# Expert weights in four wide pieces per expert through a raw ring of four slots

## The chip, the cores and the metric

The kernel runs on one core of a Trainium2 chip. The metric is the device time of one execution in microseconds. Lower is better. A core has a matrix engine (TensorE, PE), an engine for element-wise work and reductions (VectorE, DVE), one for activations (ScalarE, ACT), one for custom work (GpSimd, POOL) and one that here only issues DMAs (SyncE, SP). Each runs its own queue of instructions in order, and they meet at semaphores.

## What is computed

One layer with the norm behind each half, over 2048 tokens of width 512, in fp32:

```python
x = layernorm(x + attention(x, W_K, W_Q, W_V, W_O))      # 16 heads of 128, causal
logits = x @ gate_w.T                                    # 64 experts
gate_vals, idx = top_k(softmax(logits), 6)
xe = the tokens of each expert, at most 128              # [64, 128, 512]
h  = silu(xe @ w1.T) * (xe @ w3.T)                       # [64, 128, 352]
ye = h @ w2.T                                            # [64, 128, 512]
routed = sum over the 6 of gate_vals * ye
z  = silu(x @ sw1.T) * (x @ sw3.T) @ sw2.T               # shared expert, 704 wide
x  = layernorm(x + routed + z)
```

## The kernel before

Four stages follow each other, each with its own block of queues: attention, projection and routing, the experts, and the combination of their results. The edit lies in the third, the function `experts`.

Every fp32 matrix operand is split into a high part (rounded to the matrix engine's format) and a low part (what is left), and a product takes three passes: high by high, low by high, high by low. For weights ScalarE makes the high part with a copy (`split_piece`, L1363) and VectorE the low part with a subtraction (L1470). Both read the raw weights from a ring in SBUF, `raw` (named `w_raw` in the trace), which SP fills (L1305).

The stage has eight bodies, and each body has twelve units in the order e, e, s: two experts and one half of the shared expert for one tile of 128 tokens. So there are 32 groups of three units in all. In a unit u TensorE does this in order: it transposes h of the unit before (`turn`, L1560), computes `up` (L1584, 24 matmuls of 352 columns), transposes the tokens of the next unit if that is an expert (L1555), and computes `down` of the unit before (L1607, 9 matmuls of 512 columns). At the start of a body, unit 0's own tokens are transposed only there, ahead of its `up`.

In a unit ScalarE splits the transposed h (L1386, L1387), writes out the result of the unit before last (L1399, and the store L1402; for a finished shared tile the store L1408), then splits the first pieces of the step, does Silu (L1427), splits the transposed tokens of the next unit into `eT` (L1381), and splits the remaining pieces. VectorE follows in the same order with the low parts, and where ScalarE does Silu it multiplies the halves into `h_sb` (L1520); `eT_lo` (L1488) comes behind it. For every second shared unit it first adds the finished tile (L1465). `up` waits for `eT_lo` and for the last up piece of its expert (`w_lo`), `turn` waits for `h_sb`, and `down` waits for the last down piece.

Before, an expert has seven pieces: four up pieces of 128 x 704 words (w1 and w3 together, one for each 128 of the 512 input columns) and three down pieces of 512 columns on 128, 128 and 96 rows. They are spread over the steps of a group (e is the group's first expert) so:

```python
pieces_of_step += [[(e + 1, p) for p in UP[2:]] + [(e, p) for p in DOWN],
                   [(e + 1, p) for p in DOWN] + [(e + 2, p) for p in UP[:2]],
                   [(e + 2, p) for p in UP[2:]] + [(e + 3, p) for p in UP[:2]]]
```

The first three pieces of each step are split ahead of Silu (`mine[:3]`), the others behind the tokens. The ring has eight slots of 704 words. On SP the load of piece q waits until the subtraction of piece q - 8 is done (L1341), and in the same queue stand the loads of tokens (`rows_in`, L1315) and, for every second shared unit, of the shared half's tokens (`sT`, two of 256 KB, L1331) and of the residual (256 KB, L1337). The first six pieces (`EARLY`) are loaded before the first body. The shared expert's weights come once, in the first body, on GpSimd's queue through a ring of two slots (`s_raw`, L1294).

Of the kernel before, what the change touches and what calls it, by code (L numbers as in the profile page):

```python
# [7 lines left out]
P = 128  # L8
# [1149 lines left out]
def experts(nc, gathered_x, x1_dram, x1T_parts, w13, w2, s13, s2, y_dram, base_dram):  # L1158


    with ExitStack() as ctx:
# [16 lines left out]
        PIECES = [(2 * INTER, P)] * DT + [(DM, rows) for _, rows in INTER_TILES]  # L1178
        NP = len(PIECES)
        IT = len(INTER_TILES)  # L1180

        UP, DOWN = range(DT), range(DT, NP)
# [10 lines left out]
        SLOTS_RAW = 8  # L1196
        assert NQ % SLOTS_RAW == 0
        PER_SLOT = 16 * NQ // SLOTS_RAW

        shared_of_step = {0: range(0, DT), 1: range(DT, NP), 3: range(NP, NP + DT), 4: range(NP + DT, 2 * NP)}  # L1200

# [4 lines left out]
        raw = sb("w_raw4", [P, SLOTS_RAW, 2 * INTER])  # L1206
# [60 lines left out]
        def dst_of(part, n, p, up, down):  # L1267

            rows = PIECES[p][1]
            return up[part][:, n, p, :] if p < DT else down[part][0:rows, n, p - DT, :]  # L1270

        def weights(up_src, down_src, p):

            rows = PIECES[p][1]
            if p < DT:
                return up_src[:, :, p, :].rearrange("a p n -> (a p) n")
            first = INTER_TILES[p - DT][0]
            return down_src[:, first:first + rows, :].rearrange("a p n -> (a p) n")

        def raw_of(buffer, slot, p):  # L1280
            cols, rows = PIECES[p]
            return buffer[0:rows, slot, 0:cols]

        @block.gpsimd
        def _(pool):
            nc.gpsimd.memset(ident[:], 0.0).then_inc(pool_step, 1)
            pool.wait_ge(pool_step, 1)
            nc.gpsimd.affine_select(out=ident[:], in_=ident[:], compare_op=ALU.not_equal, fill=1.0,
                                    base=0, pattern=[[-1, P]], channel_multiplier=1).then_inc(pool_const, 1)
            for k in range(SHARED_PARTS * NP):  # L1290
                half, p = k // NP, k % NP
                if k >= 2:
                    pool.wait_ge(s_lo, k - 1)
                pool.dma_start(raw_of(s_raw, k % 2, p), weights(s13[half:half + 1], s2[half:half + 1], p)  # L1294
                               ).then_inc(s_in[k % 2], 16)

        @block.sync
        def _(sp):
# [50 lines left out]
        def _(act):  # L1349
# [7 lines left out]
            def split_piece(i, q):  # L1357
# [3 lines left out]
                act.wait_ge(up_ready if p < DT else down_ready, after(i, NU, back + 1))  # L1361
                act.wait_ge(raw_in[q % SLOTS_RAW], after(i, PER_SLOT, 16 * (q // SLOTS_RAW) + 16))
                nc.scalar.activation(dst_of(0, n % 2, p, up_w, down_w), raw_of(raw, q % SLOTS_RAW, p),  # L1363
                                     ACT.Copy).then_inc(w_hi, 1)

            def split_shared(k):
                half, p = k // NP, k % NP
                act.wait_ge(s_in[k % 2], 16 * (k // 2) + 16)
                nc.scalar.activation(dst_of(0, half, p, s_up, s_down), raw_of(s_raw, k % 2, p),
                                     ACT.Copy).then_inc(s_hi, 1)  # L1370
# [39 lines left out]
            def body(i, first):  # L1410
                for u, (kind, n) in enumerate(UNITS):
# [4 lines left out]
                    if first and u == 0:  # L1416
                        for q in EARLY[DT:]:
                            split_piece(-1, q)
# [3 lines left out]
                    for q in mine[:3]:  # L1422
                        split_piece(i, q)
# [6 lines left out]
                    for q in mine[3:]:  # L1430
# [5 lines left out]
            for q in EARLY[:DT]:  # L1436
# [12 lines left out]
        def _(dve):  # L1449
# [17 lines left out]
            def split_piece(i, q):  # L1467
                n, p = pieces[q]
                dve.wait_ge(w_hi, after(i, NQ, q + 1))
                nc.vector.tensor_tensor(dst_of(1, n % 2, p, up_w, down_w), raw_of(raw, q % SLOTS_RAW, p),  # L1470
                                        dst_of(0, n % 2, p, up_w, down_w).bitcast(F32),
                                        ALU.subtract).then_inc(w_lo, 1)

            def split_shared(k):
                half, p = k // NP, k % NP
                dve.wait_ge(s_hi, k + 1)
                nc.vector.tensor_tensor(dst_of(1, half, p, s_up, s_down), raw_of(s_raw, k % 2, p),
                                        dst_of(0, half, p, s_up, s_down).bitcast(F32),
                                        ALU.subtract).then_inc(s_lo, 1)
# [17 lines left out]
            def body(i, first):  # L1497
                for u, (kind, n) in enumerate(UNITS):
# [4 lines left out]
                    if first and u == 0:  # L1503
                        for q in EARLY[DT:]:
# [4 lines left out]
                    for q in mine[:3]:  # L1509
# [14 lines left out]
                    for q in mine[3:]:  # L1524
# [5 lines left out]
            for q in EARLY[:DT]:  # L1530
# [8 lines left out]
        def _(pe):  # L1539
# [24 lines left out]
            def up(i, u, first_body):  # L1564
# [3 lines left out]
                if kind == "e":  # L1568

                    pe.wait_ge(t_lo, after(i, NT, t_at["x", u]))  # L1570
                    pe.wait_ge(w_lo, after(i, NQ, piece_at(n, DT - 1) + 1))
                    lhs = [eT[m][:, n % 2] for m in range(2)]
                    rhs = [up_w[m][:, n % 2] for m in range(2)]
                else:
                    s = n // 2
                    pe.wait_ge(sT_loaded[s % 2], i * (32 * NS // 4) + (32 * (s // 2) + 32))
                    if first_body:
                        pe.wait_ge(s_lo, NP * (n % 2) + DT)
# [11 lines left out]
            def down(i, u, wrapped, first_body=False):  # L1590
# [8 lines left out]
                else:  # L1599
                    s = n // 2  # L1600
                    pe.wait_ge(ys_read, after(i, NS // 2, s - (NS // 2 if wrapped else 0)))
                    if first_body:
                        pe.wait_ge(s_lo, NP * (n % 2 + 1))
# [254 lines left out]
def lay_out(name, a, np):  # L1858
# [17 lines left out]
    if name == "w2":  # L1876
        return a["L0_ffn_w2"].transpose(0, 2, 1)
# [23 lines left out]
```

## Time and profile before

| | us |
|---|---|
| time, median of 3 runs | 2947.56 |
| lowest and highest run | 2942.06, 2953.83 |
| span of the profiled execution, first to last instruction | 2943.9 |
| expert stage, within the span | about 2101 to 2790 |
| TensorE busy in the span | 2531.6 |
| VectorE, ScalarE busy in the span | 1937.3, 1497.5 |

The span is that of one execution under the profiler. No separate device time of that execution is given, so the median of the runs stands beside it. Busy times are summed over stages with different limits, so they say little about one stage.

### The profile page before, as it was taken

What the parts mean: (1) busy time and instruction counts of PE and PEld (TensorE: products, weight loads), DVE (VectorE), ACT (ScalarE), POOL (GpSimd) and SP (SyncE); (2) the same over time, 40 slices, a digit from 0 to 9 for tenths busy, and PEclk for the clock granted to TensorE, in tenths of its full rate; (3) what the DMA queues carried; (4) which work ended last, traced back from release to release, by engine and by line L of the source; (5) the groups of instructions that cost most, each with busy time, mean ns of one, the idle gap of its engine ahead of it and who ended that gap; (6) DMA issues with size and microseconds to landing.
All of it is one profiled execution on the core that took longest, in us unless ns stands there. A gap on an engine that the chain in (4) does not pass through costs nothing. (4 is left out here: it accounts for less than half of the span.)

```text
span 2943.9 us, 49114 instructions
## 1 busy us (share of the span) xinstructions
PE 2531.6 (86%) x14224; PEld 2162.2 (73%) x14224; DVE 1937.3 (66%) x4447; ACT 1497.5 (51%) x3302; POOL 213.4 (7%) x222
## 2 busy tenths in 40 slices
PE   6998998998998998998998997988289999999800
PEld 5877877876887886887887885766279999999800
DVE  5675665664675665665665665778467777777766
ACT  4553553553553554554554454443256676766612
POOL 0000000000000000000000000244200000000076
PEclk9999999999999999999999999999589999999955
DMA  6211211211211211221121122675478888888773
GB/s 238 88 55 54 88 55 54 88 55 50 90 56 50 87 60 50 79 66 52 62 76 59 54 84 107 220 237 180 148 239 288 288 298 299 287 299 290 249 233 101
DMA packets 213219, 405.71 MB, mean 138 GB/s; under 512 B 23234, under 2 KB 88898, under 8 KB 202480
## 3 DMA queue, kind: packets, MB, share of 16 engines
q1 hardware_dynamic: 148912, 322.95, 33.0%
q10 hardware_dynamic: 47616, 41.95, 4.2%
q0 software_dynamic: 16448, 37.93, 4.0%
q8 instruction: 108, 1.77, 0.2%
q14 instruction: 135, 1.11, 0.1%
HBM read 314.64 MB, written 104.86 MB: 142 GB/s over the span
## 5 line engine op out<-in xcount | busy, mean ns | idle before, releaser
L404 ACT ACTIVATE pT_hi<-turned 128x512 fp32r<-128x512 f32 (+3 forms) x640 | 335.1, 534 | 393.3 <-PE turned L656 391.9
L393 ACT ACTIVATE probs<-bank,neg_max 128x512 f32<-128x512 f32 (+3 forms) x640 | 394.6, 627 | 170.9 <-DVE neg_max L517 170.0
L552 DVE TENSOR_TENSOR pT_lo<-turned,pT_hi 128x512 fp32r<-128x512 f32 (+3 forms) x640 | 374.6, 606 | 99.7 <-ACT pT_hi L404 99.7
L511 DVE TENSOR_REDUCE max_part<-bank 128x1 f32<-128x512 f32 (+3 forms) x640 | 363.4, 605 | 25.8 <-PE bank L609 12.1
L620 PE MATMUL bank<-x_sb,w_hi 128*128 128x512 f32 x1056 | 339.6, 404 | 37.9 <-DMA x_sb<-x_parts 24.5
L656 PE MATMUL turned<-ident,probs 128*128 128x128 f32 x2176 | 331.8, 273 | 37.9 <-ACT probs L393 37.9
L656 PEld LDWEIGHTS turned<-ident,probs 128*128 128x128 f32 x2176 | 262.5, 140 | 89.5 <-ACT probs L393 41.0
L672 PE MATMUL z_ps<-pT_hi,v_hi 128*128 128x512 f32 (+3 forms) x640 | 277.2, 433 | 48.7 <-DVE pT_lo L552 47.8
L1470 DVE TENSOR_TENSOR up_lo<-w_raw,up_hi 128x704 fp32r<-128x704 f32 x262 | 221.7, 887 | 107.9 <-ACT up_hi L1363 106.9
L620 PEld LDWEIGHTS bank<-x_sb,w_hi 128*128 128x128 f32 x1056 | 203.7, 195 | 82.5 <-DMA x_sb<-x_parts 25.6
L638 PE MATMUL bank<-k_lo,q_hi 128*128 128x512 f32 (+2 forms) x640 | 253.6, 396 | 0.0
L638 PE MATMUL bank<-k_hi,q_hi 128*128 128x512 f32 (+2 forms) x640 | 238.9, 373 | 12.8 <-ACT probs L393 12.8
L672 PE MATMUL z_ps<-pT_hi,v_lo 128*128 128x512 f32 (+3 forms) x640 | 233.8, 365 | 0.0
L638 PE MATMUL bank<-k_hi,q_lo 128*128 128x512 f32 (+2 forms) x640 | 233.0, 364 | 0.0
L672 PE MATMUL z_ps<-pT_lo,v_hi 128*128 128x512 f32 (+3 forms) x640 | 232.9, 364 | 0.0
L1363 ACT ACTIVATE up_hi<-w_raw 128x704 fp32r<-128x704 f32 x262 | 192.7, 783 | 73.5 <-ACT y_sb L1399 38.6
L620 PE MATMUL bank<-x_sb,w_lo 128*128 128x512 f32 x528 | 212.0, 402 | 0.0
L609 PE MATMUL bank<-w_hi,x_sb 128*128 128x256 f32 x1024 | 198.6, 287 | 0.5
L1584 PE MATMUL h_ps<-up_hi,eT_hi 128*128 128x352 f32 x512 | 172.0, 336 | 19.4 <-DVE eT_lo L1488 19.1
L672 PEld LDWEIGHTS z_ps<-pT_hi,v_hi 128*128 128x128 f32 x640 | 120.9, 189 | 76.6 <-DVE pT_lo L552 53.7
L609 PEld LDWEIGHTS bank<-w_hi,x_sb 128*128 128x128 f32 x1024 | 165.9, 194 | 3.6 <-ACT probs L393 2.9
L1584 PE MATMUL h_ps<-up_lo,eT_hi 128*128 128x352 f32 x512 | 166.6, 325 | 0.0
(182 smaller groups left out, 5200.0 us busy)
## 6 DMA issues: line engine op xcount, KB each, us to landing
w_raw<-in_w SPq DMA_DIRECT2D x262, 352.0 KB, 5.0
x_sb<-x_parts SPq DMA_DIRECT2D x64, 1024.0 KB, 7.7
w_raw<-in_w SPq DMA_DIRECT2D x128, 256.0 KB, 4.7
rows_in<-gathered_x SPq DMA_DIRECT2D x65, 256.0 KB, 4.4
gathered_x<-zeros SPq DMA_DIRECT2D x64, 256.0 KB, 8.1
z_dram<-z_sb ACTq DMA_DIRECT2D x64, 256.0 KB, 2.3
z_raw<-z_dram SPq DMA_DIRECT2D x16, 1024.0 KB, 6.5
y_dram<-y_sb ACTq DMA_DIRECT2D x64, 256.0 KB, 3.7
```

Of the source, the lines that this page charges most:

```text
L393: nc.scalar.activation(probs[:, u % 2, r, kc * CHUNK:kc * CHUNK + used], bank[:, job_at["s", h, c, r, kc] % BANKS, 0:used], ACT.Exp, bias= ...
L404: nc.scalar.activation(pT_sb[0][:, n % TURNS, lo_col:], turned[:, n % TURNS, lo_col:], ACT.Copy).then_inc(turn_hi, 1)
L511: nc.vector.reduce_max(dst, bank[:, job_at[job] % BANKS, 0:used], axis=AX_X).then_inc(part_done, 1)
L552: nc.vector.tensor_tensor(pT_sb[1][:, n % TURNS, lo_col:], turned[:, n % TURNS, lo_col:], pT_sb[0][:, n % TURNS, lo_col:].bitcast(F32), AL ...
L609: mark = nc.tensor.matmul(dst[:, t * 2 * DH:(t + 1) * 2 * DH], x_sb[:, a, dt, rows_], w_sb[b][:, dt, 4 * DH:], start=(dt == 0 and (a, b) = ...
L620: mark = nc.tensor.matmul(dst, w_sb[a][:, dt, first:first + DH], x_sb[:, b, dt, :], start=(dt == 0 and (a, b) == PASSES[0]), stop=(dt == D ...
L638: mark = nc.tensor.matmul(dst[:, 0:width], q_sb[a][:, h, r * P:(r + 1) * P], k_sb[b][:, h, kc * CHUNK:kc * CHUNK + width], start=(a, b) == ...
L656: mark = nc.tensor.transpose(turned[:, n % TURNS, r * P:(r + 1) * P], probs[:, u % 2, r, j * P:(j + 1) * P], ident[:])
L672: mark = nc.tensor.matmul(z_ps[:, first * P:], v_sb[a][:, j, h * DH:(h + 1) * DH], pT_sb[b][:, n % TURNS, first * P:], start=(j == 0 and ( ...
L1363: nc.scalar.activation(dst_of(0, n % 2, p, up_w, down_w), raw_of(raw, q % SLOTS_RAW, p), ACT.Copy).then_inc(w_hi, 1)
L1470: nc.vector.tensor_tensor(dst_of(1, n % 2, p, up_w, down_w), raw_of(raw, q % SLOTS_RAW, p), dst_of(0, n % 2, p, up_w, down_w).bitcast(F32) ...
L1584: mark = nc.tensor.matmul(h_ps[:, u % 2, k, 0:INTER], lhs[a][:, d * P:(d + 1) * P], rhs[b][:, d, k * INTER:(k + 1) * INTER], start=d == 0 ...
```

## The change

An expert's weights now come in four pieces: two up pieces of 128 x 1408 words (two old ones side by side), one down piece of 128 x 1024 (the first two down tiles side by side), and the down piece of 96 x 512 as before. The array w2 is laid out anew on the host, so that the wide down piece is one contiguous row for each partition. The ring has four slots of 1408 words, which is the same memory as before. A load now waits for the subtraction four pieces back. The steps of a group hold three, three and two pieces. The first two of each step are split ahead of Silu (`BEFORE_SILU`), so in the shared unit's step both stand ahead of it. `EARLY` is now three pieces. The shared expert's pieces keep their sizes, under names of their own.

```diff
-        PIECES = [(2 * INTER, P)] * DT + [(DM, rows) for _, rows in INTER_TILES]
+        IT = len(INTER_TILES)
+        UP_PIECES = DT // 2
+        PIECES = [(4 * INTER, P)] * UP_PIECES + [(2 * DM, P), (DM, INTER_TILES[-1][1])]
...
+        SHARED_PIECES = [(2 * INTER, P)] * DT + [(DM, rows) for _, rows in INTER_TILES]
+        NSP = len(SHARED_PIECES)
+
+        UP0, UP1, DOWN0, DOWN1 = range(NP)
         pieces_of_step = []
         for e in range(0, NE, 2):
-            pieces_of_step += [[(e + 1, p) for p in UP[2:]] + [(e, p) for p in DOWN],
-                               [(e + 1, p) for p in DOWN] + [(e + 2, p) for p in UP[:2]],
-                               [(e + 2, p) for p in UP[2:]] + [(e + 3, p) for p in UP[:2]]]
+            pieces_of_step += [[(e + 1, UP1), (e, DOWN0), (e, DOWN1)],
+                               [(e + 1, DOWN0), (e + 1, DOWN1), (e + 2, UP0)],
+                               [(e + 2, UP1), (e + 3, UP0)]]
+        BEFORE_SILU = 2
...
-        SLOTS_RAW = 8
+        SLOTS_RAW = 4
...
-        raw = sb("w_raw4", [P, SLOTS_RAW, 2 * INTER])
+        raw = sb("w_raw4", [P, SLOTS_RAW, 4 * INTER])
...
+        def expert_weights(e, p):
+
+            if p < UP_PIECES:
+                return w13[bass.ds(e, 1), :, 2 * p:2 * p + 2, :].rearrange("a p t n -> (a p) (t n)")
+            first = 0 if p == DOWN0 else 2 * P * DM
+            cols, rows = PIECES[p]
+            return w2[bass.ds(e, 1), first:first + rows * cols].rearrange("a (p n) -> (a p) n", n=cols)
...
-                sp.dma_start(raw_of(raw, q % SLOTS_RAW, p), weights(w13[bass.ds(e, 1)], w2[bass.ds(e, 1)], p)
-                             ).then_inc(raw_in[q % SLOTS_RAW], 16)
+                sp.dma_start(raw_of(q % SLOTS_RAW, p), expert_weights(e, p)).then_inc(raw_in[q % SLOTS_RAW], 16)
...
-                    for q in mine[:3]:
+                    for q in mine[:BEFORE_SILU]:
                         split_piece(i, q)
...
-            for q in EARLY[:DT]:
+            for q in EARLY[:UP_PIECES]:
                 split_piece(-1, q)
...
-                    pe.wait_ge(w_lo, after(i, NQ, piece_at(n, DT - 1) + 1))
+                    pe.wait_ge(w_lo, after(i, NQ, piece_at(n, UP_PIECES - 1) + 1))
...
-        return a["L0_ffn_w2"].transpose(0, 2, 1)
+        w = a["L0_ffn_w2"].transpose(0, 2, 1)
+        pairs = w[:, :2 * P].reshape(EXPERTS, 2, P, DM).transpose(0, 2, 1, 3).reshape(EXPERTS, 2 * P * DM)
+        return np.concatenate([pairs, w[:, 2 * P:].reshape(EXPERTS, -1)], 1)
```

## Rows read from the trace of the kernel before

**Rows 1.** Busy time of each engine in three stretches of the expert stage

```profile
core 0: us, PE busy (x) PEld busy (x) DVE busy (x) ACT busy (x) POOL busy (x), PEclk, DMA share, GB/s
2100.00:2200.00 100.00, 65.89 (x316) 58.30 (x316) 55.74 (x89) 51.98 (x95) 8.12 (x16) 0.79 0.73 243
2110.00:2120.00 10.00, 6.09 (x24) 6.12 (x25) 7.26 (x9) 7.42 (x10) 0.00 (x0) 0.55 1.05 357
2400.00:2500.00 100.00, 98.39 (x582) 91.36 (x582) 74.79 (x129) 69.54 (x135) 0.00 (x0) 1.00 0.88 295
```

**Rows 2.** Waits of TensorE, 2200 to 2700: total us, times, longest

```profile
PE h_ps L1584 <- DVE eT_lo L1488: 9.7, 6, 1.6
```

**Rows 3.** Timeline of ScalarE: start us, us, line, what, idle before

```profile
2401.78 2.15 ACT L1363 ACTIVATE up_hi<-w_raw 128x704 fp32r<-128x704 f32 x3 [0.60 <-ACT y_sb L1399]
2403.98 0.47 ACT L1427 ACTIVATE act_sb<-h_ps 128x352 f32<-128x352 f32 x1
...
2408.48 1.48 ACT L1363 ACTIVATE up_hi<-w_raw 128x704 fp32r<-128x704 f32 x2 [0.61 <-ACT y_sb L1399]
...
2410.68 0.47 ACT L1427 ACTIVATE act_sb<-h_ps 128x352 f32<-128x352 f32 x1 [0.20 <-PE h_ps L1584]
...
2417.36 0.46 ACT L1427 ACTIVATE act_sb<-h_ps 128x352 f32<-128x352 f32 x1 [1.72 <-PE h_ps L1584]
...
2421.43 2.15 ACT L1363 ACTIVATE up_hi<-w_raw 128x704 fp32r<-128x704 f32 x3 [0.63 <-ACT y_sb L1399]
```

**Rows 4.** Timeline of VectorE

```profile
2402.60 2.50 DVE L1470 TENSOR_TENSOR up_lo<-w_raw,up_hi 128x704 fp32r<-128x704 f32 x3 [1.17 <-ACT up_hi L1363]
2405.01 0.52 DVE L1520 TENSOR_TENSOR h_sb<-act_sb,h_ps 128x352 f32<-128x352 f32 x1
2405.44 0.69 DVE L1488 TENSOR_TENSOR eT_lo<-t_ps,eT_hi 128x512 fp32r<-128x512 f32 x1
...
2409.31 1.70 DVE L1470 TENSOR_TENSOR up_lo<-w_raw,up_hi 128x704 fp32r<-128x704 f32 x2 [1.28 <-ACT up_hi L1363]
...
2411.95 0.68 DVE L1488 TENSOR_TENSOR eT_lo<-t_ps,eT_hi 128x512 fp32r<-128x512 f32 x1
...
2438.04 0.51 DVE L1520 TENSOR_TENSOR h_sb<-act_sb,h_ps 128x352 f32<-128x352 f32 x1
...
2463.92 0.52 DVE L1520 TENSOR_TENSOR h_sb<-act_sb,h_ps 128x352 f32<-128x352 f32 x1
```

**Rows 5.** Timeline of TensorE's weight loads

```profile
2406.08 0.47 PEld L1560 LDWEIGHTS t_ps<-ident,h_sb 128*128 128x128 f32 x3
2406.53 0.19 PEld L1584 LDWEIGHTS h_ps<-up_hi,eT_hi 128*128 128x128 f32 x1
...
2412.78 0.47 PEld L1560 LDWEIGHTS t_ps<-ident,h_sb 128*128 128x128 f32 x3
2413.23 0.19 PEld L1584 LDWEIGHTS h_ps<-up_hi,eT_hi 128*128 128x128 f32 x1
...
2438.66 0.47 PEld L1560 LDWEIGHTS t_ps<-ident,h_sb 128*128 128x128 f32 x3
...
2464.53 0.47 PEld L1560 LDWEIGHTS t_ps<-ident,h_sb 128*128 128x128 f32 x3
```

**Rows 6.** Groups by line, shapes apart: count, busy us, mean ns, idle before

```profile
L886 ACT ACTIVATE z_hi<-z_raw 128x2048 fp32r<-128x2048 f32 x16 | 30.4, 1901 | 10.7 <-DMA z_raw<-z_dram 10.7
L878 ACT ACTIVATE wo_hi<-wo_raw 128x1024 fp32r<-128x1024 f32 x8 | 8.5, 1058 | 1.4 <-DMA wo_raw<-in_w_o 1.3
...
L1024 DVE TENSOR_TENSOR z_lo<-z_raw,z_hi 128x2048 fp32r<-128x2048 f32 x16 | 36.6, 2286 | 8.3 <-ACT z_hi L886 8.2
L1019 DVE TENSOR_TENSOR wo_lo<-wo_raw,wo_hi 128x1024 fp32r<-128x1024 f32 x8 | 9.2, 1221 | 0.0
```

**Rows 7.** DMA issues: count, KB each, median us from issue to landing

```profile
w_raw<-in_w SPq DMA_DIRECT2D x262, 352.0 KB, 5.0
```

**Rows 8.** Timeline of TensorE, the first up of the stage

```profile
2113.91 0.63 PE L1584 MATMUL h_ps<-up_hi,eT_hi 128*128 128x352 f32 x1 [7.87 <-DVE eT_lo L1488]
```

More of the change, by code:

```diff
@@ L1265, in job_before, with dst_of, raw_of, shared_dst_of @@
             return n == 0
[L1267 to L1274, printed above, removed]
-            if p < DT:
[L1276 to L1282, printed above, removed]
+        def dst_of(part, n, p):
+            if p < UP_PIECES:
+                return up_w[part][:, n, 2 * p:2 * p + 2, :].rearrange("p t n -> p (t n)")
+            if p == DOWN0:
+                return down_w[part][:, n, 0:2, :].rearrange("p t n -> p (t n)")
+            return down_w[part][0:PIECES[p][1], n, IT - 1, :]
+        def raw_of(slot, p):
+            cols, rows = PIECES[p]
+            return raw[0:rows, slot, 0:cols]
+        def expert_weights(e, p):
+            if p < UP_PIECES:
+                return w13[bass.ds(e, 1), :, 2 * p:2 * p + 2, :].rearrange("a p t n -> (a p) (t n)")
+            first = 0 if p == DOWN0 else 2 * P * DM
+            cols, rows = PIECES[p]
+            return w2[bass.ds(e, 1), first:first + rows * cols].rearrange("a (p n) -> (a p) n", n=cols)
+        def shared_dst_of(part, half, p):
+            rows = SHARED_PIECES[p][1]
+            return s_up[part][:, half, p, :] if p < DT else s_down[part][0:rows, half, p - DT, :]
+        def shared_raw_of(slot, p):
+            cols, rows = SHARED_PIECES[p]
+            return s_raw[0:rows, slot, 0:cols]
+        def shared_weights(half, p):
+            if p < DT:
+                return s13[half:half + 1, :, p, :].rearrange("a p n -> (a p) n")
+            first, rows = INTER_TILES[p - DT]
+            return s2[half:half + 1, first:first + rows, :].rearrange("a p n -> (a p) n")
         @block.gpsimd
@@ L1289, in _ @@
                                     base=0, pattern=[[-1, P]], channel_multiplier=1).then_inc(pool_const, 1)
-            for k in range(SHARED_PARTS * NP):
-                half, p = k // NP, k % NP
+            for k in range(SHARED_PARTS * NSP):
+                half, p = k // NSP, k % NSP
                 if k >= 2:
                     pool.wait_ge(s_lo, k - 1)
-                pool.dma_start(raw_of(s_raw, k % 2, p), weights(s13[half:half + 1], s2[half:half + 1], p)
-                               ).then_inc(s_in[k % 2], 16)
+                pool.dma_start(shared_raw_of(k % 2, p), shared_weights(half, p)).then_inc(s_in[k % 2], 16)
         @block.sync
@@ L1429, in body @@
                         turned(i, ("x", u + 1))
-                    for q in mine[3:]:
+                    for q in mine[BEFORE_SILU:]:
                         split_piece(i, q)
@@ L1523, in body @@
                         turned(i, ("x", u + 1))
-                    for q in mine[3:]:
+                    for q in mine[BEFORE_SILU:]:
                         split_piece(i, q)
@@ L1528, in body @@
                             split_shared(k)
-            for q in EARLY[:DT]:
+            for q in EARLY[:UP_PIECES]:
                 split_piece(-1, q)
```

36 lines of the change are left out of this document (15 added, 21 removed).

## The prediction

> **What bounds the kernel now.** The edit touches only the expert stage, which lies between 2101 us and 2790 us of the span, so I read the table of stretches first. In a settled stretch of that stage TensorE is busy 98.4 of 100 us at a granted clock of 1.00, VectorE 74.8 and ScalarE 69.5, and the DMA engines are busy 0.88 of the time at 295 GB/s [rows 1]. The first 100 us are different: TensorE is busy 65.9 us of them [rows 1]. The waits of TensorE between 2200 and 2700 us come next: six waits of up to 1.6 us, all on the low half of the transposed tokens, 9.7 us in total [rows 2]. That is one per body. So TensorE sets the pace and can get no faster by more than those waits; what the edit can do in the settled part is put waits where there are none. I therefore read the timelines of ScalarE, VectorE and TensorE's weight loads over one group of three units (two experts and one shared half, 32 groups in all), and asked how late each result may come before TensorE misses it.
>
> **The margins.** Unit s (shared) first. ScalarE starts its three 704-wide copies at 2401.78 and runs Silu at 2403.98, right behind them [rows 3]. VectorE starts their three subtractions at 2402.60, starts h_sb at 2405.01 and eT_lo at 2405.44, which ends at 2406.13 [rows 4]. TensorE loads h_sb at 2406.08 and the first weights of the next up at 2406.53 [rows 5]. From a result to the load that waits for it I take 0.09 us: at the end of a body h_sb ends at 2463.92 + 0.52 = 2464.44 [rows 4] and is loaded at 2464.53 [rows 5]. So h_sb has 0.46 us to spare in unit s and eT_lo 0.31. In the first expert unit eT_lo ends at 2412.63 [rows 4] for a load at 2413.23 [rows 5]: 0.51 to spare. In the second expert unit ScalarE stands idle 1.72 us before Silu [rows 3], a wide margin, except where a finished shared tile is added first (every second group): there h_sb ends at 2438.55 [rows 4] for a load at 2438.66 [rows 5], nothing to spare. The end of a body has nothing to spare either, as the 0.09 above shows.
>
> **Price of the wide operations.** The trace has 1024- and 2048-wide ones of the same kinds: ScalarE 1.058 and 1.901 us, VectorE 1.221 and 2.286 us [rows 6]. Interpolated, 1408 columns cost ScalarE 1.37 and VectorE 1.62 us. A queued operation starts about 0.1 us before the end of the one ahead: two subtractions take 1.70 and three 2.50, so 0.80 each against 0.90 for one alone [rows 4]; ScalarE's two take 1.48 and three 2.15 [rows 3]. Merging thus saves about 0.07 us of ScalarE and 0.08 of VectorE per pair. No engine that sets the pace gets that. What counts is that VectorE may begin only when the first copy is whole, 1.37 us after it starts and not the 0.81 of a narrow one (1.48 less the 0.67 that a further copy adds), and that unit s now has two wide pieces (four old ones) ahead of Silu and h_sb where it had three old ones.
>
> The Trainium skill's page Perfetto Trace Analysis, section Optimizing Scalar/DVE Operations, states both sides: larger operations help throughput if the engine is saturated, while engines that are not saturated but leave gaps on others may finish sooner with instructions broken up. By its first half the sum below would be a small gain, by its second a loss; the busy shares of VectorE and ScalarE [rows 1] put this stage under the second.
>
> **Unit s, step by step.** First copy 2401.78 to 2403.15. First subtraction 2403.19 to 2404.81; the second copy is done at 2404.42, so the second subtraction runs 2404.71 to 2406.33. h_sb follows, 2406.24 to 2406.76, 1.23 later than before; eT_lo 2406.67 to 2407.36. TensorE loads h_sb at 2406.85 (0.77 late) and begins the next up at 2407.45, against 2406.53: **0.92 us** lost.
>
> **First expert unit.** Its ScalarE work starts from the transposes that are 0.77 late: the copies begin at 2408.48 [rows 3] + 0.77 = 2409.25. One 1408-wide piece and the 1024-wide down piece stand ahead of Silu. Copy to 2410.62, subtraction 2410.66 to 2412.28, the down piece's 2412.18 to 2413.40, h_sb 2413.31 to 2413.83, eT_lo 2413.74 to 2414.42. Silu, due at 2410.68 [rows 3] + 0.92, is not held up. TensorE, due at 2412.78 + 0.92 for h_sb, gets it at 2413.92, and the up that was at 2413.23 starts at 2414.51. That is 1.28 late in all: **0.36 us** more.
>
> **Second expert unit.** The 1.72 us of idle time cover the 1024-wide copy and its subtraction: nothing. Without that cover it would be the groups with a finished tile: on the line of [rows 6] a 512-wide copy is 0.64 and a subtraction 0.69, so the first copy is 0.42 longer than it was and the two subtractions 0.08 shorter than the three; h_sb comes 0.34 later, and TensorE, itself 0.14 later after eT_lo in the middle of a body, loses 0.20 there and 0.34 behind the end of a body. At the end of a body, with no margin, unit s loses 1.23, and the expert unit behind it, whose tokens are transposed only there, loses nothing.
>
> **Sum of the settled part.** A body has three groups at 1.28, one at 1.23, and 0.20 + 0.34: 5.6 us, times eight 45 us. The first body spends its first half waiting for the shared weights, whose pieces and ring of two slots do not change; I take off half a body, 3 us. TensorE's first up waited for eT_lo [rows 8], which stands behind the last up piece on VectorE: a 1408-wide piece after the last landing costs 0.56 + 0.72 = 1.3 us more than a 704-wide one. That is 43 us.
>
> **The ring.** Four slots hold one expert, eight held a little more. Each load waits for the subtraction four pieces back. By the times above (group now 19.65 us, from 2401.78 to 2421.43 [rows 3], + 1.3 to 1.4), with everything counted from one s unit to the next, the wide load ahead of unit s goes out at 2413.5 (behind the subtraction that ends at 2413.40), its own two at about 2415.1 (behind the last down piece, which follows eT_lo) and 2417.5 (behind the next unit's first down piece, a copy and a subtraction some 1.1 us late); these two are wanted at 2422.8 and 2424.1. Bytes in order from 2413.5: 0.72 MB, tokens 0.26, in every second group the shared half's 0.79, then 0.72 and 0.72, with 0.26 of stores between. At the highest rate that a row shows, 357 GB/s [rows 1], or at 295/0.88 = 335, the second of them ends after 7.7 to 8.2 us and the third after 9.7 to 10.4, and some 1 us passes before a transfer is seen. So in every second group the wide loads are 0 to 1.5 us late; in the others (0.79 MB less) they are in time. On ScalarE, Silu and the next tokens' copy stand behind a late piece, and on VectorE h_sb and eT_lo, so it delays unit s in full. On SP's queue the next token load stands behind a waiting weight load; it is wanted a unit or more later and is priced at nothing, or at the same lateness if that cover were gone. Sixteen groups at 0 to 1.5 us are 0 to 24; I take 0.5 each, **8 us**, nearer to the lower end because the slower group gives the DMA 6% more time. The median says much the same: a 352 KB load lands in 5.0 us [rows 7], 0.36 MB more at 335 GB/s makes 6.1, against windows of 7.7 and 6.6.
>
> Before, a load went out eight pieces ahead and the waits of TensorE show no late weights [rows 2]. Fewer packets (5632-byte rows for 2816) I price at nothing: the stage is not paced by them.
>
> Total 43 + 8 = 51 us. The profiled span is 2943.9 us and the median of the runs 2947.56; the 3.7 us between them I leave as they are. **Forecast 2999 us.** Less than 0.5%, 15 us, is no change here.
>
> **Rivals.** *The ring becomes the bound.* If loads of 704 KB are late in all groups, not in half of them, by 1.5 us, that is 30 x 1.5 = 45 us in place of 8: about 3036 us. For it: 0.88 busy DMA engines [rows 1] and the loss of lookahead. Against it: the odd groups carry 0.79 MB less. The Trainium skill (Perfetto Trace Analysis, Optimization Strategy) says that a gap repeated on the engine that should be saturated can mean too few buffers; no row of before shows such a gap.
>
> *No change.* The queues may hide the whole of it if the wide operations start their consumers sooner than I think. Bound: VectorE's and ScalarE's fixed cost vanishes, 1408 columns at the slope of the wide rows being 1.16 and 1.46 us. That takes 0.5 off unit s and 0.36 off the expert unit, leaving 0.4 a group: 30 x 0.4 + 1.3 on 2947.6 is 2961 us with nothing from the ring. Only a margin that I misread by another 0.4 us gives 2948. For it, nothing but the smallness of the margins.
>
> *Faster.* TensorE stands still 34 of the first 100 us [rows 1], in part for weights. If wide rows raise the transfer rate there, where the DMA engines are busy 1.05 [rows 1], and half of that comes back while the settled part keeps its pace, the time is 2948 - 17 = 2931. It decides only if over 15 us of the 34 return. Against it: the shared weights come through their own unchanged ring. The Trainium skill (DMA: Bandwidth & Descriptors, Rules for kernel authors) advises large transfers of 1 MiB and more for bandwidth, which is this direction; no row of before shows weights in both sizes.
>
> **How the numbers follow.** Chances: forecast 0.68, ring as the bound 0.20, no change 0.08, faster 0.04. The lower end of the range is the cheap bound, rounded to 2962; if wide pieces cost what two narrow ones do (1.6 and 1.77), a group loses some 0.8 more, 24 us, and 2999 + 24 is 3023; the ring's case reaches 3036 and a little past it with both. Range 2962 to 3042, which leaves out the two lesser cases and the worst of the ring.
>
> **What would show it.** In the profile after: waits of TensorE of about 0.9 us in front of the first up behind each shared unit and of 0.2 to 0.4 in the expert unit behind it, both put down to h_sb or eT_lo; TensorE's share of a settled 100 us near 92; VectorE's wide subtraction near 1.62 us and ScalarE's copy near 1.37; waits of ScalarE on weights in transit only in every second group. It is wrong if TensorE stays above 98, or if those waits on weights appear in all groups, or if the start moves by more than some us.

## The result, and the profile after

The changed kernel takes 3019.44 us (median of 4 runs, 3016.35 to 3026.13). The kernel before takes 2948.55 beside it. The ratio is 1.0241, with a 95% interval of 1.0222 to 1.026: 71 us slower. The forecast was 2999 us, in a range of 2962 to 3042.

To place the 71 us I cut both spans at two rows: GpSimd's memset of `ident`, which opens the expert stage, and TensorE's last matmul of that stage. These are the two in the timeline of the changed kernel:

```profile
2095.19 0.20 POOL L1307 MEMSET ident<- 128x128 f32 x1 [9.48 <-POOLq L704]
...
2853.86 0.39 PE L1622 MATMUL ys_ps<-s_down_hi,hT_lo 96*128 96x512 f32 x1
```

The same two rows in the profile of before:

```profile
2101.53 0.20 POOL L1286 MEMSET ident<- 128x128 f32 x1 [9.49 <-POOLq L704]
...
2790.03 0.40 PE L1607 MATMUL ys_ps<-s_down_hi,hT_lo 96*128 96x512 f32 x1
```

The expert stage takes 2853.86 - 2095.19 = 758.7 us. Before it takes 2790.03 - 2101.53 = 688.5 us. So the stage is 70.2 us longer, and the edit touches nothing else. The combine stage, from that row to the end of the span, took 153.9 us before and 160.7 after, but the last experiment shows that this part varies by itself. Where experiments are compared below I therefore give the expert stage beside the median.

The table of stretches of the changed kernel (columns as in [rows 1]):

```profile
2400.00:2500.00 100.00, 92.62 (x510) 83.44 (x509) 64.83 (x88) 59.85 (x96) 0.00 (x0) 0.96 0.77 264
2200.00:2700.00 500.00, 465.03 (x2580) 418.83 (x2579) 326.96 (x435) 297.08 (x470) 0.00 (x0) 0.97 0.76 265
```

TensorE was busy 98.39 of the 100 us from 2400 [rows 1]. Now it is 92.62, near the forecast 92. The DMA engines fall from 0.88 to 0.77, so the memory is less used, not more. The first body, from the memset to the first weight load of the second body, takes 131.8 us (2227.00 - 2095.19) where it took 121.8 (2223.37 - 2101.53).

Waits in the changed kernel, 2200 to 2700 (total us, times, longest):

```profile
PE t_ps L1575 <- DVE h_sb L1535: 23.5, 23, 2.6
...
ACT up_hi L1382 <- DMA w_raw<-in_w: 17.4, 16, 2.4
PE h_ps L1599 <- DVE eT_lo L1503: 9.7, 6, 1.6
```

The 9.7 us on `eT_lo` were there before [rows 2]. New are the waits for `h_sb`, and behind some of them a wait of ScalarE for weights in transit. The wide operations cost what was forecast (1.62 and 1.37), by the groups of the whole span:

```profile
L1487 DVE TENSOR_TENSOR up_lo<-w_raw,up_hi 128x1408 fp32r<-128x1408 f32 x131 | 211.0, 1623 | 160.9 <-ACT up_hi L1382 159.8
...
L1382 ACT ACTIVATE up_hi<-w_raw 128x1408 fp32r<-128x1408 f32 x131 | 178.4, 1376 | 90.1 <-DMA w_raw<-in_w 56.8
```

TensorE's timeline shows where the waits stand in one body. These are the rows of 2400 to 2480 with an idle time ahead:

```profile
2406.62 0.55 PE L1575 MATMUL t_ps<-ident,h_sb 128*128 128x128 f32 x3 [0.84 <-DVE h_sb L1535]
2409.22 0.42 PE L1599 MATMUL h_ps<-up_hi,eT_hi 128*128 128x352 f32 x1 [1.61 <-DVE eT_lo L1503]
...
2430.92 0.55 PE L1575 MATMUL t_ps<-ident,h_sb 128*128 128x128 f32 x3 [0.38 <-DVE h_sb L1535]
...
2451.77 0.55 PE L1575 MATMUL t_ps<-ident,h_sb 128*128 128x128 f32 x3 [0.38 <-DVE h_sb L1535]
...
2473.56 0.55 PE L1575 MATMUL t_ps<-ident,h_sb 128*128 128x128 f32 x3 [1.34 <-DVE h_sb L1535]
```

The first two rows are the end of a body: 0.84 is new, 1.61 is the old wait. The next two follow a shared unit whose weights came in time, and the last one a shared unit whose weights came late. Such late units stand in every second group, those with a shared tile to load and to finish (the first and the third of a body). Of ScalarE's 16 waits for weights only one, of 0.45 us at the end of the first body, stands in another group.

**The late group.** The queue of SP (start, time, line), first in the group without a finished tile, then in the next one, which has it:

```profile
2439.14 0.33 SPq L1325 DMA_DIRECT2D w_raw<-in_w  x1
2441.52 0.33 SPq L1325 DMA_DIRECT2D w_raw<-in_w  x1
...
2459.54 0.85 SPq L1350 DMA_DIRECT2D sT<-x1T_parts  x2
2460.59 0.33 SPq L1356 DMA_DIRECT2D ys_sb<-x_dram  x1
2461.17 0.33 SPq L1325 DMA_DIRECT2D w_raw<-in_w  x1
2464.34 0.33 SPq L1325 DMA_DIRECT2D w_raw<-in_w  x1
```

ScalarE's timeline, its copies for the shared unit of either group and the down copies ahead of the second:

```profile
2446.71 2.65 ACT L1382 ACTIVATE up_hi<-w_raw 128x1408 fp32r<-128x1408 f32 x2 [0.61 <-ACT y_sb L1416]
...
2461.85 1.58 ACT L1382 ACTIVATE down_hi<-w_raw 128x1024 fp32r<-128x1024 f32 x2 [1.86 <-DVE ys_sb L1482]
...
2468.29 1.38 ACT L1382 ACTIVATE up_hi<-w_raw 128x1408 fp32r<-128x1408 f32 x1 [1.36 <-DMA w_raw<-in_w]
2470.03 1.39 ACT L1382 ACTIVATE up_hi<-w_raw 128x1408 fp32r<-128x1408 f32 x1 [0.36 <-DMA w_raw<-in_w]
```

VectorE's timeline, the two subtractions that free the slots in the second group:

```profile
2459.14 0.68 DVE L1487 TENSOR_TENSOR down_lo<-w_raw,down_hi 96x512 fp32r<-96x512 f32 x1
...
2462.94 1.82 DVE L1487 TENSOR_TENSOR down_lo<-w_raw,down_hi 128x1024 fp32r<-128x1024 f32 x2 [1.70 <-ACT down_hi L1382]
```

The shared unit needs two wide pieces. Without a tile they go out at 2439.14 and 2441.52 and are copied from 2446.71, the second about 1.3 us later: 7.6 and 6.5 us of time to land. With a tile, the first one's slot is free at 2459.14 + 0.68 = 2459.82, but on SP the three loads for the shared tile stand ahead, and it goes out at 2461.17. The second one's slot waits for a down piece whose copy stands behind the tile's addition (1.86 us idle on `ys_sb`), and it goes out at 2464.34. ScalarE is ready for the first at 2468.29 - 1.36 = 2466.93 and for the second some 1.3 us later. That leaves 5.8 and 3.9 us. Their copies start 7.1 and 5.7 us after the loads went out. The median time to land is 5.9 (DMA issues, 2200 to 2700, of the changed kernel):

```profile
w_raw<-in_w SPq DMA_DIRECT2D x88, 704.0 KB, 5.9
```

The DMA queues over the same 20 us (2455 to 2475 of the changed kernel, slices of 0.5 us, busy tenths):

```profile
DMA  3000003869789899999989999999999999999777
```

The same view of before, over a group with a tile (2434 to 2454):

```profile
DMA  9999989899999999999999999999998519599999
```

Now the DMA engines stand still for about 2.5 us, because all four slots are full and SP waits for a subtraction, and must then bring the tile and the wide pieces all at once. Eight slots kept them evenly busy.

### The profile page after: what moved, and what is told of

It is laid out like the page before. It is cut to its first block and busy times, and to the rows that moved or that the text cites. A ratio compares the mean times of both kernels' runs of the same rounds, so it can differ in the third digit from the quotient of the medians.

```text
span 3014.6 us, 47584 instructions
## 1 busy us (share of the span) xinstructions
PE 2565.2 (85%) x14224; PEld 2175.3 (72%) x14224; DVE 1926.9 (64%) x4252; ACT 1475.3 (49%) x3107; POOL 209.9 (7%) x222
## 5 line engine op out<-in xcount | busy, mean ns | idle before, releaser
L1487 DVE TENSOR_TENSOR up_lo<-w_raw,up_hi 128x1408 fp32r<-128x1408 f32 x131 | 211.0, 1623 | 160.9 <-ACT up_hi L1382 159.8
L1382 ACT ACTIVATE up_hi<-w_raw 128x1408 fp32r<-128x1408 f32 x131 | 178.4, 1376 | 90.1 <-DMA w_raw<-in_w 56.8
L1599 PE MATMUL h_ps<-up_hi,eT_hi 128*128 128x352 f32 x512 | 180.4, 352 | 21.8 <-DVE eT_lo L1503 19.1
L1599 PE MATMUL h_ps<-up_lo,eT_hi 128*128 128x352 f32 x512 | 173.7, 339 | 0.0
L1599 PE MATMUL h_ps<-up_hi,eT_lo 128*128 128x352 f32 x512 | 173.0, 338 | 0.0
```

The source lines that it names most:

```text
L1382: nc.scalar.activation(dst_of(0, n % 2, p), raw_of(q % SLOTS_RAW, p), ACT.Copy).then_inc(w_hi, 1)
L1487: nc.vector.tensor_tensor(dst_of(1, n % 2, p), raw_of(q % SLOTS_RAW, p), dst_of(0, n % 2, p).bitcast(F32), ALU.subtract).then_inc(w_lo, 1)
L1599: mark = nc.tensor.matmul(h_ps[:, u % 2, k, 0:INTER], lhs[a][:, d * P:(d + 1) * P], rhs[b][:, d, k * INTER:(k + 1) * INTER], start=d == 0 ...
```

## The experiments

At the start three causes stood against each other: the chain of wide splits ahead of `h_sb`, as forecast (A), the ring of four slots that recycles too late (B), and larger transfers that are slower by themselves (C). A fourth came up with the profile: TensorE's granted clock falls behind the new waits, which might cost something of its own. Later expectations use the letters for their own pair of theories and say which. The diffs are against the changed kernel.

**narrow_split: wide loads, splits in the old halves, three ahead of Silu.**

```diff
-        BEFORE_SILU = 2
+        BEFORE_SILU = 3
...
-                nc.scalar.activation(dst_of(0, n % 2, p), raw_of(q % SLOTS_RAW, p), ACT.Copy).then_inc(w_hi, 1)
+                nc.scalar.activation(half(dst_of(0, n % 2, p), q, part), half(raw_of(q % SLOTS_RAW, p), q, part),
+                                     ACT.Copy).then_inc(w_hi, 1)
...
```

> The four wide loads and the ring of four slots stay, but ScalarE and VectorE split each piece in its old halves (704 or 512 columns), three of them ahead of Silu as before the change. Theory A (the wide copies and subtractions ahead of h_sb make TensorE wait; the ring adds some 10 us; what is left is TensorE's lower clock after the longest waits): 2960 us, plus or minus 10, the settled TensorE share back at 97 or more. Theory B (four slots recycle too late, whatever the width of the splits): 3010 to 3025. Theory C (a 704 KB transfer lands later than two of 352 KB): also 3010 to 3025.

2990.25 us, ratio to before 1.0143 (1.0115 to 1.0172). All theories missed. The waits of this kernel, 2200 to 2700:

```profile
ACT up_hi L1398 <- DMA w_raw<-in_w: 38.5, 29, 3.0
...
PE h_ps L1617 <- DMA sT<-x1T_parts: 12.7, 11, 1.5
...
PE t_ps L1593 <- DVE h_sb L1553: 1.7, 3, 1.1
```

The wait for `h_sb` is gone (1.7 us for 23.5), so the wide splits make it. But the ring of four slots alone still costs 39 us, and not the few that I had taken. The shared unit's tokens (`sT`) are late too: they stand on SP behind loads that wait for slots.

**two_dma: each piece in two transfers of half the size.**

```diff
-                sp.dma_start(raw_of(q % SLOTS_RAW, p), expert_weights(e, p)).then_inc(raw_in[q % SLOTS_RAW], 16)
+                for part in range(2):
...
+                        sp.dma_start(dst[:, a:b], src[:, a:b]).then_inc(raw_in[q % SLOTS_RAW], 16)
```

> As the changed kernel, with wide splits and four slots, but each piece comes in two transfers of half the size (by columns; the 96-row piece in two times 48 rows). Theories A and B: as the changed kernel, 3019 us within 8. Theory C: under 2990.

3023.39 us, 1.0248 (1.0216 to 1.028): no better than whole pieces, as A and B expected. C is out.

**deep_ring: eight slots of 1408 words.** The room comes from the shared up weights, whose low part is put on top of the high part, which changes the shared expert's values.

```diff
-        SLOTS_RAW = 4
+        SLOTS_RAW = 8
...
-        s_up = [sb(f"s_up_{n}", [P, SHARED_PARTS, DT, 2 * INTER], F32R) for n in ("hi", "lo")]
+        s_up = [sb("s_up_hi", [P, SHARED_PARTS, DT, 2 * INTER], F32R)] * 2
```

> As the changed kernel, but eight slots of 1408 words. The room comes from keeping the low part of the shared expert's up weights in the place of the high part, so the shared expert's result lacks its high part; no operation is left out. Theory A: no load is late any more, the waits of about 1.5 us in every second group fall to 0.4, with them about half of the falls of the clock: 2997 us, plus or minus 8. Theory B: 2960 or less. Theory C: 3010 or more.

2996.71 us, 1.0164 (1.0135 to 1.0192): the time that A expected. ScalarE no longer waits for weights anywhere between 2200 and 2700. The granted clock there is 1.00, so all falls of the clock are gone and not half of them. What is left is the chain, in its timeline of TensorE's weight loads over one group:

```profile
2424.49 0.29 PEld L1575 LDWEIGHTS t_ps<-ident,h_sb 128*128 128x128 f32 x3 [0.82 <-DVE h_sb L1535]
...
2437.87 0.47 PEld L1575 LDWEIGHTS t_ps<-ident,h_sb 128*128 128x128 f32 x3
...
2445.34 0.29 PEld L1575 LDWEIGHTS t_ps<-ident,h_sb 128*128 128x128 f32 x3 [0.81 <-DVE h_sb L1535]
```

A group takes 20.85 us for the 19.65 of before: 1.20 more, where the forecast had 1.28.

**one_before: one, two and one wide pieces ahead of Silu** in the three steps of a group, so that `h_sb` is no later than it was.

```diff
-        BEFORE_SILU = 2
+        BEFORE_SILU = (1, 2, 1)
...
-                    for q in mine[:BEFORE_SILU]:
+                    for q in mine[:BEFORE_SILU[u % 3]]:
...
```

> As the changed kernel, but in the steps of unit s and of the first expert unit only one wide piece is split ahead of Silu, the others behind the next tokens (in the second expert unit two, as they are). Theory A: h_sb and eT_lo come in time again, 2955 us, plus or minus 10, and late loads no longer reach h_sb through the second piece. Theories B and C: 3005 or more, since the ring and the transfers are the same.

3015.62 us, 1.0229 (1.0189 to 1.0268): a miss for A, and in the range of B. A piece that is split later frees its slot later. From the waits of 2200 to 2700:

```profile
ACT up_hi L1382 <- DMA w_raw<-in_w: 54.0, 39, 4.3
...
PE t_ps L1575 <- DVE h_sb L1535: 3.2, 12, 0.3
```

The chain's waits went, and the ring's took their place.

**filler: matmuls with no use in TensorE's waits**, so that its granted clock does not fall: nine behind each shared unit and eighteen at the start of a body, into a part of PSUM that nothing reads.

```diff
+                    if not first and u % 3 == 0:
+                        fill(u, 9)
...
+                        if not first:
+                            fill(u, 18)
```

> As the changed kernel, but from the second body on TensorE does 9 matmuls of 160 columns ahead of the transposes of h behind each shared unit, and 18 ahead of the first up of a body, into columns of h_ps that nobody reads: work added in its waits, nothing left out. Theory A (part of the loss is TensorE's lower clock after its longest waits): the granted clock of 2200 to 2700 us goes from 0.97 to 0.99 or more and the time falls by 10 to 20, to 3000 to 3010 us. Rival (the clock falls only while TensorE would wait anyway): the clock rises too, the time stays at 3019 us within 5 or grows by the added work.

3016.3 us, 1.0218 (1.0182 to 1.0255): the time stays, as the rival expected. The stretch of the changed kernel behind the waits at the start of a body, then the five bodies of this one:

```profile
2410.00:2413.00 3.00, 3.00 (x12) 3.00 (x11) 2.14 (x2) 1.77 (x2) 0.00 (x0) 0.50 0.18 67
```

```profile
2200.00:2700.00 500.00, 486.63 (x2907) 445.40 (x2906) 328.94 (x438) 296.67 (x473) 0.00 (x0) 1.00 0.77 267
```

Behind some of its waits the changed kernel runs at 1.2 GHz for some us (0.50). With filler the clock is 1.00 over the five bodies, and the time is the same within 3 us. That does not yet say that the falls cost nothing, because filler adds work and a single total can hide two changes. The groups tell them apart. In the changed kernel the last group of a body comes with a fall behind the late unit ahead of it, or without one. One group with a fall begins at the `turn` of 2473.56 above and ends at the first row here, and one without lies between the other two. The stretches show the clock at the start of either:

```profile
2495.73 0.55 PE L1575 MATMUL t_ps<-ident,h_sb 128*128 128x128 f32 x3 [0.83 <-DVE h_sb L1535]
...
2562.69 0.55 PE L1575 MATMUL t_ps<-ident,h_sb 128*128 128x128 f32 x3 [1.38 <-DVE h_sb L1535]
...
2583.50 0.55 PE L1575 MATMUL t_ps<-ident,h_sb 128*128 128x128 f32 x3 [0.83 <-DVE h_sb L1535]
```

```profile
2475.00:2481.00 6.00, 6.00 (x30) 5.84 (x30) 3.60 (x6) 3.58 (x6) 0.00 (x0) 0.76 0.40 145
2564.00:2570.00 6.00, 6.00 (x37) 5.53 (x36) 4.12 (x6) 4.20 (x6) 0.00 (x0) 1.00 0.42 152
```

With the fall the group takes 2495.73 - 2473.56 = 22.17 us, without it 20.81, so the fall costs 1.36 us. With filler every such group takes 20.8. But filler's own nine matmuls make the second group of each body longer, 21.2 us for 20.85, and in the groups with a tile the weights are still late: ScalarE waits 24.0 us for them here and 17.4 without filler. At the start of a body the changed kernel's falls are mostly hidden, because the next unit's late weights have not landed anyway: that group takes 24.3 us in two bodies with a fall and 25.4 in a third, and 24.0 to 24.3 without. So part of what the clock gave back was taken by the ring and part by the filler itself. Neither theory holds as it was put.

**early_shared: the shared tile's three loads one unit earlier on SP's queue.**

```diff
-                    if kind == "s" and n % 2 == 0:
-                        s = n // 2
+                    if u + 1 < NU and UNITS[u + 1][0] == "s" and UNITS[u + 1][1] % 2 == 0:
+                        s = UNITS[u + 1][1] // 2
```

> As the changed kernel, but on SP's queue the three loads of the shared tile (0.79 MB) stand one unit earlier, ahead of the weight loads of the second expert unit's step. If the late loads of every second group come from those bytes between the wide loads: the waits of about 1.5 us fall to 0.4, the clock stays up, 2997 us within 8, as with the deep ring. If the four slots are late by themselves: 3012 to 3025.

3012.06 us, 1.0201 (1.0177 to 1.0225), at the edge of the rival's range. The profile says more than the median: the waits for weights are 4.8 us in place of 17.4, and the expert stage is 741.6 us, 17 less than in the changed kernel. Its combine stage took 171.8 us, the longest of all, and hides part of that.

**deep_one: the edits of deep_ring and one_before together**, with the same stand-in for the low part of the shared up weights.

> Eight slots of 1408 words (the low part of the shared up weights stands in the place of the high part, so the shared result lacks it) and one wide piece ahead of Silu in unit s and the first expert unit. Theory A, as it stands now (two limits of similar size, the chain through h_sb and the ring, each of which is the bound when the other is gone): both gone, 2951 us within 6. If the moved pieces cost something of their own: 2965 or more.

2971.1 us (10 runs), 1.006 (1.0045 to 1.0075). The moved pieces cost something of their own: of the chain's 42 us in the expert stage 27 come back, 15 do not. In its profile the wait at the start of a body is 1.8 us for 1.6, and `h_sb` is 0.2 to 0.3 late twelve times in five bodies. ScalarE never waits for weights from 2200 to 2700. The first weight loads of three bodies, and a stretch at the start of the first two:

```profile
2465.51 0.47 PEld L1575 LDWEIGHTS t_ps<-ident,h_sb 128*128 128x128 f32 x3
...
2547.05 0.47 PEld L1575 LDWEIGHTS t_ps<-ident,h_sb 128*128 128x128 f32 x3
...
2630.11 0.47 PEld L1575 LDWEIGHTS t_ps<-ident,h_sb 128*128 128x128 f32 x3
```

```profile
2467.00:2476.00 9.00, 7.49 (x45) 7.03 (x46) 5.54 (x9) 5.26 (x9) 0.00 (x0) 1.00 0.90 317
2549.00:2558.00 9.00, 7.95 (x37) 7.54 (x38) 4.00 (x7) 4.08 (x6) 0.00 (x0) 0.81 0.93 319
```

The first of these bodies takes 81.54 us and the second, with a fall of the clock, 83.06. Here no late weight hides the fall, and it costs 1.5 us. The six bodies from the second to the seventh are together 10.0 us longer than before: two such falls make 3.0 of it, and 7.0 lie in the groups with a tile. The other 4.7 of the 15 lie in the first and the last body.

**narrow_early: the edits of narrow_split and early_shared together.**

> Wide loads, four slots, splits in the old halves (as the kernel narrow_split, 2990 us), and the shared tile's three loads one unit earlier on SP's queue. If the bytes between the wide loads are what is left of the loss there: 2951 to 2962 us. If the ring is late by itself: 2980 to 2995.

2970.48 us, 1.0066 (1.0043 to 1.009), between the two expectations. From its waits, 2200 to 2700:

```profile
ACT up_hi L1398 <- DMA w_raw<-in_w: 25.5, 31, 1.6
```

TensorE no longer waits for `sT`. Half of what the ring costs alone was the place of those loads on the queue. The other half stays with the slots.

**deep_narrow: the edits of narrow_split and deep_ring together**, so wide transfers, eight slots and narrow splits, with the same stand-in.

> The wide transfers of the changed kernel, but eight ring slots of 1408 words (the low part of the shared up weights stands on the high part to make room, which changes the shared expert's values) and the splits in the old halves, three ahead of Silu. It is the fourth corner of two by two: wide splits with four slots took 3019 us, wide splits with eight slots 2997, narrow splits with four slots 2990. Theory A (the whole cost lies in these two limits, and the width of the transfers costs nothing): this corner is the kernel before again, 2951 us within 6, the expert stage within 3 us of the 688.5 us of before, ScalarE waiting for weights under 1 us in the five bodies' stretch. Rival B (fewer and larger transfers, or the moved storage, cost something of their own that was put down to the ring or the chain): 2960 us or more, with waits on weight loads or a longer expert stage.

2955.44 us (10 runs), 1.0002 (0.9988 to 1.0016): the kernel before again, as A expected. Its stretch:

```profile
2400.00:2500.00 100.00, 98.39 (x582) 91.35 (x581) 74.58 (x128) 69.52 (x135) 0.00 (x0) 1.00 0.88 290
```

**before_again: the kernel before, profiled once more.**

> The kernel before, unchanged, profiled a second time. From TensorE's last instruction of the expert stage to the end, the combine stage, whose code the change leaves alone, took 153.9 us in the profile of before, 160.7 in that of the changed kernel, and 156.8 to 171.8 in those of the experiments so far. Theory A (the stage varies from run to run by itself): the second profile of before lies anywhere between 153 and 172 us, and not at 153.9 again. Rival B (the stage is longer because of something in the edited kernels): 153 to 155 us again.

2954.51 us in one run. The row that ends its expert stage, in the timeline of TensorE:

```profile
2785.09 0.39 PE L1607 MATMUL ys_ps<-s_down_hi,hT_lo 96*128 96x512 f32 x1
```

From 2097.10, its memset, the expert stage takes 688.0 us (688.5 in the first profile). From that row to the end of the span, 2952.7, are 167.6 us, where the first profile had 153.9. The same kernel's combine stage differs by 14 us. So A holds, and the 7 us between before and after say nothing of the edit.

All profiles side by side, medians of the timed runs and the two stages of the profiled one:

| kernel | splits | slots | median | expert stage | against 688.5 | combine |
|---|---|---|---|---|---|---|
| before | narrow | 8 of 704 | 2948.55 | 688.5 | | 153.9 |
| before_again | narrow | 8 of 704 | 2954.51 (one run) | 688.0 | -0.5 | 167.6 |
| deep_narrow | narrow | 8 of 1408 | 2955.44 | 690.4 | +1.9 | 164.4 |
| narrow_early | narrow, tile early | 4 | 2970.48 | 705.6 | +17.1 | 164.0 |
| narrow_split | narrow | 4 | 2990.25 | 726.1 | +37.6 | 161.6 |
| deep_one | wide, 1, 2, 1 | 8 of 1408 | 2971.10 | 703.2 | +14.7 | 170.2 |
| deep_ring | wide | 8 of 1408 | 2996.71 | 730.5 | +42.0 | 156.8 |
| early_shared | wide, tile early | 4 | 3012.06 | 741.6 | +53.1 | 171.8 |
| one_before | wide, 1, 2, 1 | 4 | 3015.62 | 751.9 | +63.4 | 158.7 |
| filler | wide | 4 | 3016.30 | 757.2 | +68.7 | 157.0 |
| changed kernel | wide | 4 | 3019.44 | 758.7 | +70.2 | 160.7 |
| two_dma | wide | 4 | 3023.39 | 764.8 | +76.3 | 161.6 |

The four corners of two widths and two rings are deep_narrow (+1.9), deep_ring (+42.0), narrow_split (+37.6) and the changed kernel (+70.2).

## Why the prediction was right, and which step of it was wrong

**What bounds the kernel.** Right. TensorE had 1.6 us in 100 to give, and the edit could only add waits. No version here is faster than before.

**The margins and unit s.** Right in mechanism and in size. The forecast had `h_sb` 0.77 us late behind the shared unit. In deep_ring the weight load of `h_sb` follows the one before by 2445.34 - 2437.87 = 7.47 us. It was 6.70 in the profile of before, 2425.71 - 2419.01:

```profile
2419.01 0.47 PEld L1560 LDWEIGHTS t_ps<-ident,h_sb 128*128 128x128 f32 x3
...
2425.71 0.47 PEld L1560 LDWEIGHTS t_ps<-ident,h_sb 128*128 128x128 f32 x3
```

That is 0.77. The remaining 0.43 of the 1.20 are split between the two other units, 0.2 each. The end of a body was to lose 1.23, and there the wait is 0.84 on TensorE's row and 1.27 on the weight load's. The 0.54 us a body for the groups with a finished tile did not come: in deep_ring the second and the third group of a body take 20.85 and 20.84 us, and only the third has a tile.

**Sum of the settled part.** Forecast 43 us, measured 42.0 in the expert stage of deep_ring, 46 by the medians (2996.71 - 2950.86). That the sum fits so well is partly luck. The first weight loads of the second and third body, in before and in deep_ring:

```profile
2223.37 0.47 PEld L1560 LDWEIGHTS t_ps<-ident,h_sb 128*128 128x128 f32 x3
...
2303.75 0.47 PEld L1560 LDWEIGHTS t_ps<-ident,h_sb 128*128 128x128 f32 x3
```

```profile
2231.42 0.29 PEld L1575 LDWEIGHTS t_ps<-ident,h_sb 128*128 128x128 f32 x3 [1.14 <-DVE h_sb L1535]
...
2316.61 0.29 PEld L1575 LDWEIGHTS t_ps<-ident,h_sb 128*128 128x128 f32 x3 [1.27 <-DVE h_sb L1535]
```

A settled body grew from 80.38 to 85.19 us, 4.8 and not the 5.6 of the forecast. The first body grew from 121.8 us (from 2101.53) to 130.3 (from the memset of deep_ring at 2101.15), 8.4 and not the 4 that half a body and the start were to cost. The two errors nearly cancel. Why the first body costs more is open; the chain is not all of it, as it is 2.0 longer in deep_narrow too. The Trainium skill says, in Perfetto Trace Analysis under Optimizing Scalar/DVE Operations, that where an engine is not saturated but leaves gaps on another, breaking up its instructions may let work finish sooner. The 42.0 us between deep_ring and before, with VectorE busy 67.06 of 100 us, agree with it, and so do the 40.1 us between deep_ring and deep_narrow, which differ only in how the pieces are split.

**The start.** Forecast 1.3 us more. From the memset to the first `up` it was 12.4 us and is 13.3 in the changed kernel: 0.9 more. The rest of the first body's 10 us comes behind it.

**The ring.** This term was mis-sized: 8 us forecast, 28.2 measured beside the chain (70.2 - 42.0), and 37.6 where the chain is not wide. The place was right, late weights in every second group with one exception. Two things were wrong in it: how late the weights are, and the clock, which the forecast left out.

The windows first. The forecast gave the two pieces of unit s 7.7 and 6.6 us to land, and in the groups without a tile they have 7.6 and 6.5. It took the same windows for the groups with a finished tile, where they are 5.8 and 3.9. Two steps stood behind that. "On SP's queue the next token load stands behind a waiting weight load ... priced at nothing" looked at tokens behind weights. The costly order was the reverse, weights behind the tile's tokens: their slot was free 1.35 us earlier. And the copy of the next down piece, which must come before its subtraction can free the last slot, stands on ScalarE behind the tile's addition (1.86 us). Loading the tile one unit earlier takes 17.1 of the 28.2 us away (early_shared), and 20.5 of the 37.6 (narrow_early).

From the second body to the seventh the changed kernel takes 24.1 us more than deep_ring. The groups with a tile hold 16.8 of them, 1.4 us each (the fall at the start of the second body among them): inside the forecast's own bounds of 0 to 1.5, but near the upper one, where it took 0.5. Its sum did not reach that upper bound: 2413.5 + 10.4 + 1 against 2424.1 is 0.8 us. The other 7.3 us lie in groups without a tile, where no weight is late and the clock is down behind a late unit, 0.9 to 1.4 us each. Of the 11 us that early_shared still has over deep_ring, the third groups of the same bodies hold 4.4, as their weights are still late, and four groups with a fall of the clock hold 5.3. That this last lateness is the down piece behind the addition fits the rows but was not tried.

**The rivals.** The ring as the bound in all groups did not come, but for the one exception in 16 waits. The forecast said that no row of before shows a repeated gap. TensorE's 1.6 us once a body [rows 2] is one, but it is 9.7 us in all with four slots (the changed kernel) and with eight (deep_ring), so it does not come from the slots. Nothing was hidden, and the start gave back nothing. The two limits overlap: 42.0 and 37.6 alone, 70.2 together and not 79.6, and the 70.2 hold falls of the clock that neither kernel with one limit has (1.00 from 2200 to 2700 in both). Of the 9 us that they share, the forecast had only the direction (a slower group gives the DMA more time).

**What would have shown it.** TensorE near 92: 92.62, and 465.03 / 5 = 93.0 over the five bodies. Waits on weights only in every second group: yes, but for one. Waits of 0.9 us behind the shared unit: 0.81 on the weight load, 0.38 on the matmul behind it. The start was not to move by more than some us: its first `up` moved by 0.9, its first body grew by 10. That falls of the clock would follow was not foreseen, and some of them cost 0.9 to 1.4 us each.

## What to carry to other kernels

Merging operations saves a fixed cost on each engine, but the next engine gets its first data only when the whole of the first operation is done: ask how many hundred nanoseconds the last consumer has to spare, not how busy the engines are. A ring with the same bytes in fewer and larger slots looks ahead less, and its loads start in bunches: work out the time from a slot's release to the next use in the busiest group of the loop, with all that stands ahead on the issuing queue, not in the group that is easiest to read. Two limits of like size hide each other, so undo both, one at a time, before blaming either. And compare the lengths of like groups, not only the total: a repair that adds work of its own can leave the total where it was.

## What the runs showed of the hardware

The same two waits of TensorE at the end of a body, 0.84 and 1.61 us, were followed by a granted clock of 0.50 in the changed kernel (2410 to 2413, above) and by 1.00 in deep_ring (2405 to 2408). From these rows the length of a wait alone does not tell whether the clock falls. What a fall costs depends on what waits behind it: 1.36 us where no late weight followed (22.17 for 20.81 us in the changed kernel), 1.5 us in deep_one (83.06 for 81.54), and 0.3 us or less at the start of two of the changed kernel's bodies (24.3 us for 24.0 to 24.3), where late weights set the time.

The kernel gained nothing from weights that were cut differently: with the same splits and slots it took 3023 us with two transfers of half the size and 3019 with whole pieces.

The combine stage, whose code is the same in all kernels, took 153.9 to 171.8 us over twelve profiles, 14 us apart for one and the same kernel. The medians carry part of this spread, so small differences between two versions are better read from the expert stage of the profiles.
